# PixArt attention with a routed feed-forward: another order of TensorE's work in a half quarter, two of VectorE's groups one unit later, three small GpSimd ops left out

## The chip, the cores and the metric

The kernel runs on one core of a Trainium2 chip (trn2). The time is device microseconds of one execution. Engines are named as in the profile: PE (TensorE matmul), PEld (its weight loads), DVE (VectorE), ACT (ScalarE), POOL (GpSimd), SP (SyncE, which here issues DMAs).

## The reference, cut to what matters

There are 16 batches of 128 x 512 numbers. The first part is attention with 8 heads over the 512 positions, with keys and values both from `ctx`; the second is a feed-forward with 8 experts of which each token takes two.

```python
s = SCALE * jnp.log(k_length)[:, None, None, None]
attn = jnp.einsum('bhdq,bhdk->bhqk', qh, kh)
attn = jax.nn.softmax(s * attn, axis=-1)
out = jnp.einsum('bhqk,bhdk->bhdq', attn, vh)
...
x = x + _L0_xcond_ref(_layernorm(x, axis=-1), ctx_2048, ctx_2048, itok_B_779_1933)
x = x + _L0_ffn_ref(_layernorm(x, axis=-1), gate_w, w1, w2, w3)
```

`_layernorm` subtracts the mean of a row and divides by its standard deviation. Here x has the shape 16 x 128 x 512, HD = 128 channels, 8 heads of 16 channels, and 512 positions for queries and keys.

## The kernel before, in words

The program has two parts in time: attention for all 16 batches up to about 530 us, then the experts, tile by tile of 128 tokens. The change lies in the first.

Attention runs as a pipeline of **slots**, one per batch b (b = -3 to 17; 4 to 11 are in a hardware loop with two slots to a pass). In slot b PE computes the scores of batch b, and around it each engine prepares or finishes others: POOL splits queries of b+2 and keys of b+3 into bfloat16 parts, which go to DRAM and come back stacked; it finishes x1 (x plus attention) of b-1; it sends the tokens of b-2 to the experts' slots; and it splits one chunk of the first expert's weights.

A slot has four **quarters** (w = 0 to 3) of eight scores (u = 0 to 7), so a **half quarter** has four scores. What PE issues in a slot, all in the loop at L1096 to L1158:
- 16 **units of rows** (`rows_unit`, L1050 to L1063): two matmuls of 96 rows by 512 into `rows` (two buffers of two banks). A unit i belongs to k = (i + 4) % 16 of the next batch, from i = 12 on of the one after it. DVE takes the maximum over the keys of each row (`maxima`, L773), and unit i may start only when the maxima of unit i-2 are done. Unit 4 and unit 12 first wait for a reload (L243) of the stacked parts.
- 32 **scores** (L1076), each 128 x 512 into one of two banks; ACT takes their exponent (L655), and a score waits for the exp of the score two before it.
- 8 groups of **values** (L1089): four float32 matmuls on 32 columns each, of the quarter before.
- small products in `misc`: the transposes of z (L1109), the gate's scores (L1116), the transposes for V (L1131), u (L1139), the ranks (L1146 to L1148), and the transpose of the maxima (L1155), which waits for the maxima of unit 11.

Every engine has its own instruction queue in program order, written out by hand; semaphores alone tie them. What stands around the change:
- DVE's queue in a slot: maxima of the 16 units, and between them the routing of b-2, the reciprocal of the softmax sums (`rden`, L808, behind unit 5), the statistics of x of b+3 (L816), the copies of the maxima (`mrow`, L873, L875, behind unit 11), and `bn_stats` and `bn_aggr` of `us` (L883, L889, behind unit 13), which wait for x1 from POOL.
- POOL's queue in a slot: `psc` (L459 to L462: the scale and the negated mean of batch b+2), `norm` (L468, L470) and its split (L436, L437), a weight chunk (L434, L437, and L483, the load of another), the keys' split, the tokens of b-2 (L503 to L512), then `us` times the reciprocals (L525), x1 (L528), the wait for DVE's statistics, `zsc` (L537 to L539) and z (L540). z of one slot is followed by `psc` of the next.
- SP's queue in a slot: the reload of half 1 (for unit 4), x and ctx loads, the keys' stores, the sums' round trip through DRAM (`sums`, `den`), the queries' stores, the store of the reciprocals, the reload of half 0 (for unit 12; it waits for the 16th score), `rb` (the reciprocals spread over the heads), the maxima's round trip, and `cv`.

ACT's queue has the exps and at the end of a slot the copy of x1 (L702), which waits for POOL's L528.

`ENGINE_STEPS` (L19) tells how many steps of POOL a semaphore counts in a slot.

Of the kernel before, what the change touches and what calls it, by code (L numbers as in the profile page):

```python
# [7 lines left out]
ALU = mybir.AluOpType  # L8
# [7 lines left out]
P = 128  # L16
LOOP_FIRST, LOOP_LAST = 2, 6
LEAD = 4
ENGINE_STEPS = {"prep": 10, "keys": 4, "z": 4, "route_a": 3, "route_b": 3}  # L19
# [39 lines left out]
def build(nc, x, ctx_kv, lengths, wpack, gate_t, out):  # L59
    B, HD, L = x.shape  # L60
# [4 lines left out]
    D = L  # L65
# [25 lines left out]
    with ExitStack() as cx:  # L91
# [10 lines left out]
        xres = sb("xres", [P, B, L], F32)  # L102
# [21 lines left out]
        us = sb("us", [P, L], F32)  # L124
        rb = sb("rb", [P, L], F32)
        z = sb("z", [P, 2, ROW], F32)
        zt = sb("zt", [P, KD, P], F32)
        selu = sb("selu", [P, 2, P], F32)
        den = sb("den", [P, 32], F32)
# [267 lines left out]
        def _(pool):  # L397
# [49 lines left out]
            def slot(b):  # L447
                pbt = b.plus(2)
                if pbt.within(0, B - 1):
# [12 lines left out]
                    st.step(g.tensor_scalar(psc[:, 3:4], mean, -1.0, 0.0, ALU.mult, ALU.add))  # L462
# [4 lines left out]
                if pbt.within(1, B - 1):  # L467
                    st.step(g.tensor_tensor(norm[:, :], xres[:, bass.ds(pbt.n, 1), :].rearrange("p o q -> p (o q)"),  # L468
                                            psc[:, 3:4].to_broadcast([P, L]), ALU.add))
# [52 lines left out]
                if pv.within(0, B - 1):  # L522
# [16 lines left out]
                    st.step(g.tensor_scalar(zsc[:, 2:3], mv2[:, 0:1], -1.0, 0.0, ALU.mult, ALU.add))  # L539
                    st.step(g.tensor_scalar(z[:, pv.parity, 0:D], us[:, :], zsc[:, 2:3], zsc[:, 1:2], ALU.add, ALU.mult))  # L540
# [199 lines left out]
        def _(dve):  # L740
# [20 lines left out]
            def slot(b):  # L761
# [42 lines left out]
                if pv.within(0, B - 1):  # L804
                    dve.wait_ge(S["den_in"], b.n * 16)
                    if pv.within(1, B - 1):
                        dve.wait_ge(S["rec_out"], b.n * 16 - 16)
                    v.reciprocal(rden[:, :], den[:, :]).then_inc(S["rec_ready"], 1)  # L808
# [12 lines left out]
                maxima(range(6, 8))  # L821
# [31 lines left out]
                if b.within(-3, -3):  # L853
# [3 lines left out]
                    q_steps.step(v.tensor_scalar(us[:, :], xres[:, 0, :], psc[:, 3:4], psc[:, 2:3], ALU.add, ALU.mult))  # L857
# [5 lines left out]
                    v.nop().then_inc(S["prep_steps"], ENGINE_STEPS["prep"] - 4)  # L863
# [13 lines left out]
                maxima(range(12, 13))  # L877
                maxima(range(13, 14))
# [11 lines left out]
                maxima(range(14, 15))  # L890
# [149 lines left out]
        def _(pe):  # L1040
# [4 lines left out]
            def slot(b):  # L1045
# [53 lines left out]
                for w in range(4):  # L1099
                    for u in range(8):  # L1100
                        if u % 4 == 0:
                            rows_unit(4 * w + u // 2)
# [17 lines left out]
                        if u in (1, 5):  # L1120
                            kk = u // 4
                            if w == 0 and behind:
                                values(pv, 3, kk)
                            if w > 0 and full:
                                values(b, w - 1, kk)
# [31 lines left out]
                        if u % 4 == 3:  # L1157
                            rows_unit(4 * w + u // 2)  # L1158
# [122 lines left out]
```

## Time and profile before

| what | value |
|---|---|
| median of 3 runs (lowest, highest) | 1180.6 us (1180.52, 1184.16) |
| the profiled execution: its own time | 1181.91 us |
| the profiled execution: span | 1180.4 us, granted TensorE clock 0.957 |
| busy over the span: PE, PEld, DVE | 1039.7, 415.4, 685.0 us |
| busy over the span: ACT, POOL | 426.6, 653.9 us |
| maxima (DVE L773), 256 | 304.9 us, 1219 ns each |
| exps (ACT L655), 512 | 283.5 us, 596 ns each |

A page of the profile tells busy time of each engine, the chain of work that ended last, and groups of instructions by line. Busy time of PE is modelled: consecutive matmuls overlap, so the time from one start to the next tells more than the duration. A bracket such as [0.70 <-DVE nm L773] behind a row of the timeline is idle time of that engine just before the instruction, and what ended it.

### The profile page before, as it was taken

To read this page: it belongs to the slowest core of one execution; us is meant where nothing else is said; L and a number is where in the kernel's file an instruction comes from. 1 tells how busy PE (TensorE), PEld (TensorE's weight loads), DVE (VectorE), ACT (ScalarE), POOL (GpSimd) and SP (SyncE) were. 2 spreads that over 40 slices of the span, in tenths; PEclk is the share of its full clock that TensorE was granted. 3 is DMA by queue.
4 is the path that set the end of the run, shared out by engine and by line. 5 is a ranking of instruction groups with operands and counts; after the bars stand their busy time and mean duration, and the time that the engine had idled before them with its cause. 6 is when DMAs were issued, how large, how long until landed. Compare 5 with 4: busy or idle time off the path is not lost.

```text
span 1180.4 us, 20555 instructions
## 1 busy us (share of the span) xinstructions
PE 1039.7 (88%) x5098; PEld 415.4 (35%) x5099; DVE 685.0 (58%) x1029; ACT 426.6 (36%) x751; POOL 653.9 (55%) x618
## 2 busy tenths in 40 slices
PE   1899998989898999871799999999999999999980
PEld 0223333323232333220344444444444444444430
DVE  5867777767776777414354546535464455543356
ACT  8267776767676777751111111111101111111110
POOL 5454777676767675223287806618384383810475
PEclk9799999999999999995899999999999999999995
DMA  6575656666656554002797755737676475843778
GB/s 192 166 217 151 189 177 175 180 180 181 180 167 185 151 169 135 30 31 68 201 229 183 208 161 146 222 89 216 175 189 193 98 206 152 227 89 81 167 191 283
DMA packets 212715, 195.70 MB, mean 166 GB/s; under 512 B 137376, under 2 KB 176288, under 8 KB 207264
## 3 DMA queue, kind: packets, MB, share of 16 engines
q1 hardware_dynamic: 197760, 122.26, 40.4%
q0 software_dynamic: 14336, 71.87, 18.7%
q10 hardware_dynamic: 576, 1.05, 0.3%
q8 instruction: 19, 0.31, 0.1%
q14 instruction: 24, 0.20, 0.0%
HBM read 111.48 MB, written 53.00 MB: 139 GB/s over the span
## 4 chain that ended last, share of the span: by engine, by line
PE 66%; DMA 11%; issue 7%; POOL 6%; DVE 6%; ACT 2%; POOLq 1%; SPq 1%; DVEq 0%
PE rows L1175 30%; PE heads_out L1175 14%; PE heads_out L1089 6%; PE scores L1076 6%; PE rows L1062 5%; DMA rb<-recips_dram 4%; DMA W<-parts_dram 4%; DVE nm L773 3%; PE misc L1139 2%; ACT W L655 1%; POOL us L525 1%; POOL us L528 1%; POOLq L595 1%; PE misc L1131 1%; POOL W L598 1%
## 5 line engine op out<-in xcount | busy, mean ns | idle before, releaser
L1175 PE MATMUL rows<-W,U 128*128 (+1 forms) x1776 | 391.5, 381 | 17.3 <-DMA U<-stage 17.0
L773 DVE TENSOR_REDUCE nm<-rows 128x2 f32<-128x1024 f32 x256 | 304.9, 1219 | 98.8 <-PE rows L1062 91.6
L655 ACT ACTIVATE W<-scores 128x512 f32<-128x512 f32 x512 | 283.5, 596 | 148.0 <-PE scores L1076 146.7
L1175 PEld LDWEIGHTS rows<-W,U 128*128 128x128 bf16 x1776 | 174.2, 98 | 228.6 <-issue 21.4
L720 ACT ACTIVATE U<-rows 128x512 f32<-128x512 f32 x78 | 46.3, 597 | 509.8 <-PE rows L1175 497.9
L1175 PE MATMUL heads_out<-W,U 128*128 x888 | 199.4, 381 | 2.3 <-DMA U<-U 2.1
L1062 PE MATMUL rows<-W,U 96*128 96x512 bf16 x512 | 148.1, 399 | 56.1 <-DMA W<-parts_dram 28.2
L980 DVE TENSOR_TENSOR U<-rows,U 128x512 bf16<-128x512 f32 x78 | 53.9, 691 | 229.2 <-ACT U L720 229.0
L1076 PE MATMUL scores<-U,W 128*128 128x512 bf16 x512 | 170.7, 390 | 5.8 <-ACT W L655 5.1
L437 POOL TENSOR_TENSOR W<-U,W 128x2048 bf16<-128x2048 f32 x42 | 171.6, 4085 | 7.7 <-POOL W L436 7.7
L436 POOL TENSOR_SCALAR W<-U 128x2048 bf16<-128x2048 f32 x42 | 80.8, 1923 | 147.6 <-PE rows L1175 139.3
L1089 PE MATMUL heads_out<-W,U 128*32 128x512 f32 x1024 | 139.4, 617 | 0.5 <-ACT W L655 0.5
L1175 PEld LDWEIGHTS heads_out<-W,U 128*128 128x128 bf16 x888 | 87.3, 98 | 108.7 <-issue 5.5
L1076 PEld LDWEIGHTS scores<-U,W 128*128 128x128 bf16 x512 | 45.6, 101 | 162.6 <-ACT W L655 131.9
L1062 PEld LDWEIGHTS rows<-W,U 96*128 96x128 bf16 x512 | 46.2, 99 | 131.6 <-DVE nm L773 57.9
L906 DVE TENSOR_TENSOR stage<-stage 128x512 bf16<-128x512 f32 x39 | 83.8, 2148 | 12.4 <-ACT stage L713 12.4
L598 POOL DMA_INDIRECT W<-expert_out_dram,fidx x24 | 24.1, 1003 | 79.3 <-issue 74.5
L984 DVE TENSOR_TENSOR rows<-rows,U 128x512 f32<-128x512 f32 x78 | 54.6, 700 | 11.6 <-DVE U L980 8.9
L988 DVE TENSOR_TENSOR U<-rows,U 128x512 bf16<-128x512 f32 x78 | 54.0, 692 | 11.7 <-DVE rows L984 8.9
L548 POOL DMA_DIRECT2D U<-wpack_dram x42 | 24.0, 572 | 41.7 <-POOL W L437 23.4
L512 POOL DMA_INDIRECT slots_dram<-z,routed x32 | 33.3, 1040 | 20.0 <-POOL chosen L506 14.1
L902 DVE TENSOR_SCALAR U<-heads_out,gates 128x512 f32<-128x512 f32 x39 | 29.3, 751 | 24.2 <-PE heads_out L1175 14.7
(170 smaller groups left out, 718.9 us busy)
## 6 DMA issues: line engine op xcount, KB each, us to landing
U<-wpack_dram POOLq DMA_DIRECT2D x42, 1024.0 KB, 5.9
parts_dram<-U SPq DMA_DIRECT2D x32, 384.0 KB, 4.1
U<-parts_dram SPq DMA_DIRECT2D x32, 384.0 KB, 4.0
W<-parts_dram SPq DMA_DIRECT2D x32, 384.0 KB, 5.1
stage<-slots_dram SPq DMA_DIRECT2D x39, 257.0 KB, 3.0
expert_out_dram<-U SPq DMA_DIRECT2D x39, 256.0 KB, 3.1
parts_dram<-U SPq DMA_DIRECT2D x32, 256.0 KB, 4.0
stage<-wpack_dram POOLq DMA_DIRECT2D x12, 512.0 KB, 6.3
```

The costliest lines, as they stand in the source:

```text
L436: steps.step(g.tensor_scalar(dst_hi, src, 1.0, 0.0, ALU.mult, ALU.add))
L437: steps.step(g.tensor_tensor(tmp if tmp is not None else dst_lo, src, dst_hi, ALU.subtract))
L655: s.activation(probs[:, w % 2, j, kk, :], sc[u % 2][:, :], ACT.Exp) \
L773: v.tensor_reduce(nm[:, bb.parity, 2 * k:2 * k + 2], p1[k % 2][:, :].rearrange("p (c k) -> p c k", c=2), AX_X, ALU.max, negate=True).then_ ...
L906: v.tensor_tensor(xb[:, 1, :], xrow[:, par, 0:D], xb[:, 0, :], ALU.subtract).then_inc(S["x_lo"], 1)
L980: v.tensor_tensor(hb[:, n, 0, :], gated, silu, ALU.mult).then_inc(S["h_hi"], 1)
L984: v.tensor_tensor(gated, gated, silu, ALU.mult).then_inc(S["h_ready"], 1)
L988: v.tensor_tensor(hb[:, n, 1, :], gated, hb[:, n, 0, :], ALU.subtract).then_inc(S["h_lo"], 1)
L1062: ins = m.matmul(p1[k % 2][:, c * 512:(c + 1) * 512], qs[0:KROWS, bb.parity, hh, q0:q0 + P], ks[0:KROWS, bb.parity, hh, :], start=True, st ...
L1076: m.matmul(sc[u % 2][:, :], ks[:, b.parity, h, kc * P:(kc + 1) * P], qs[:, b.parity, h, :], start=True, stop=True).then_inc(S["scores_read ...
L1089: ins = m.matmul(ob[32 * j:32 * j + 32, :], vt[:, bb.parity, kc, 4 * (w // 2) + j, :], probs[:, w % 2, j, kk, :], start=(kc == 0), stop=(k ...
L1175: ins = m.matmul(bank, part_of(s_part, k), W[:, bass.ds(at_w, 512)], start=(k == 0 and n == 0), stop=(k == n_chunks - 1 and n == 2))
```

## The change

It does four things.

1. PE's half quarter: before, it was unit, score, score, values, score, score, unit, and so two units stood side by side. Now it is unit, score, values, score, unit, score, score. The small products keep their places behind their scores (a product at u = 4 now comes ahead of the values).
2. DVE's reciprocal moves from behind unit 5 to behind unit 6.
3. DVE's statistics of `us` (L883, L889) move from behind unit 13 to behind unit 14.
4. POOL no longer writes the negated mean: L462 and L539 are left out, in each batch's preparation and each z, and L468, L540 and DVE's L857 subtract the mean itself. Counting the first batch's own preparation apart from the others, these are three uses.

```diff
-ENGINE_STEPS = {"prep": 10, "keys": 4, "z": 4, "route_a": 3, "route_b": 3}
+ENGINE_STEPS = {"prep": 9, "keys": 4, "z": 3, "route_a": 3, "route_b": 3}
...
-                    st.step(g.tensor_scalar(psc[:, 3:4], mean, -1.0, 0.0, ALU.mult, ALU.add))
...
                     st.step(g.tensor_tensor(norm[:, :], xres[:, bass.ds(pbt.n, 1), :].rearrange("p o q -> p (o q)"),
-                                            psc[:, 3:4].to_broadcast([P, L]), ALU.add))
+                                            mean.to_broadcast([P, L]), ALU.subtract))
...
-                    st.step(g.tensor_scalar(zsc[:, 2:3], mv2[:, 0:1], -1.0, 0.0, ALU.mult, ALU.add))
-                    st.step(g.tensor_scalar(z[:, pv.parity, 0:D], us[:, :], zsc[:, 2:3], zsc[:, 1:2], ALU.add, ALU.mult))
+                    st.step(g.tensor_scalar(z[:, pv.parity, 0:D], us[:, :], mv2[:, 0:1], zsc[:, 1:2], ALU.subtract, ALU.mult))
...
                 maxima(range(4, 6))
-                if pv.within(0, B - 1):
-                    dve.wait_ge(S["den_in"], b.n * 16)
...
-                    v.reciprocal(rden[:, :], den[:, :]).then_inc(S["rec_ready"], 1)
...
-                maxima(range(6, 8))
+                maxima(range(6, 7))
+                if pv.within(0, B - 1):
+                    dve.wait_ge(S["den_in"], b.n * 16)
...
+                    v.reciprocal(rden[:, :], den[:, :]).then_inc(S["rec_ready"], 1)
+                maxima(range(7, 8))
...
-                    q_steps.step(v.tensor_scalar(us[:, :], xres[:, 0, :], psc[:, 3:4], psc[:, 2:3], ALU.add, ALU.mult))
+                    q_steps.step(v.tensor_scalar(us[:, :], xres[:, 0, :], mv1[:, 0, 0:1], psc[:, 2:3], ALU.subtract, ALU.mult))
...
-                maxima(range(12, 13))
-                maxima(range(13, 14))
+                maxima(range(12, 15))
                 if pv.within(0, B - 1):
                     dve.wait_ge(S["x1_ready"], b.n)
...
-                maxima(range(14, 15))
                 maxima(range(15, 16))
...
                         if u % 4 == 0:
-                            rows_unit(4 * w + u // 2)
+                            rows_unit(4 * w + 2 * (u // 4))
                         if full:
                             score(w, u)
...
-                        if u in (1, 5):
-                            kk = u // 4
-                            if w == 0 and behind:
-                                values(pv, 3, kk)
-                            if w > 0 and full:
-                                values(b, w - 1, kk)
...
-                        if u % 4 == 3:
-                            rows_unit(4 * w + u // 2)
+                        if u in (0, 4):
+                            kk = u // 4
+                            if w == 0 and behind:
+                                values(pv, 3, kk)
+                            if w > 0 and full:
+                                values(b, w - 1, kk)
+                        if u % 4 == 1:
+                            rows_unit(4 * w + 2 * (u // 4) + 1)
```

PE before, around the transpose of the maxima of one slot (L1155, `nm`): units 11 and 12 side by side (the `rows` row x4), and later units 13 and 14. `scores` is L1076, `heads_out` the values.

```order
-L1076 MATMUL scores<-U,W 128x512 x2
-L1062 MATMUL rows<-W,U 128x512 x4
-L1076 MATMUL scores<-U,W 128x512
-L1155 MATMUL misc<-ident,nm 128x128
-L1076 MATMUL scores<-U,W 128x512
-L1089 MATMUL heads_out<-W,U 32x512 x4
-L1076 MATMUL scores<-U,W 128x512 x2
-L1062 MATMUL rows<-W,U 128x512 x4
-L1076 MATMUL scores<-U,W 128x512 x2
```

PE now, at the same place (the lines are those of the changed file: L1073 scores, L1059 rows, L1086 values, L1146 the transpose):

```order
+L1059 MATMUL rows<-W,U 128x512 x2
+L1073 MATMUL scores<-U,W 128x512 x2
+L1059 MATMUL rows<-W,U 128x512 x2
+L1073 MATMUL scores<-U,W 128x512
+L1146 MATMUL misc<-ident,nm 128x128
+L1086 MATMUL heads_out<-W,U 32x512 x4
+L1073 MATMUL scores<-U,W 128x512
+L1059 MATMUL rows<-W,U 128x512 x2
+L1073 MATMUL scores<-U,W 128x512 x2
+L1059 MATMUL rows<-W,U 128x512 x2
```

No two units stand side by side any more: two scores are between unit 11 and unit 12, and values between the first score of a half and its second.

DVE before, from the copies of the maxima (`mrow`) on; the two reductions ahead of BN_STATS are units 12 and 13, those behind it unit 14 and on:

```order
-L875 TENSOR_TENSOR mrow<-misc,mrow 32x128
-L771 REGISTER_ALU
-L772 ISA
-L773 TENSOR_REDUCE nm<-rows 128x2
-L772 REGISTER_ALU
-L773 TENSOR_REDUCE nm<-rows 128x2
-L883 BN_STATS st<-us 128x6
-L889 BN_AGGR mv<-st 128x2
-L772 REGISTER_ALU
-L773 TENSOR_REDUCE nm<-rows 128x2
```

DVE now:

```order
+L874 TENSOR_TENSOR mrow<-misc,mrow 32x128
+L769 REGISTER_ALU
+L770 ISA
+L771 TENSOR_REDUCE nm<-rows 128x2
+L770 REGISTER_ALU
+L771 TENSOR_REDUCE nm<-rows 128x2
+L770 REGISTER_ALU
+L771 TENSOR_REDUCE nm<-rows 128x2
+L881 BN_STATS st<-us 128x6
+L887 BN_AGGR mv<-st 128x2
```

One more reduction stands ahead of the statistics.

## Rows read from the trace of the kernel before

**Rows 1.** Windows: us, busy us (instructions) of each engine, granted clock, DMA share, GB/s.

```profile
core 0: us, PE busy (x) PEld busy (x) DVE busy (x) ACT busy (x) POOL busy (x), PEclk, DMA share, GB/s
180.00:405.00 225.00, 203.16 (x1111) 68.62 (x1112) 163.43 (x222) 151.94 (x286) 157.00 (x201) 0.98 0.60 175
```

**Rows 2.** Waits in 101 to 405: who <- for whom: us, times, longest.

```profile
PE rows L1062 <- DVE nm L773: 17.8, 19, 1.8
POOL zsc L537 <- DVE mv L889: 17.7, 10, 3.6
```

**Rows 3.** Timeline, PE: start, us, instruction, [idle before <- releaser]. Slots 7 to 9.

```profile
286.38 0.61 PE L1062 MATMUL rows<-W,U 96*128 96x512 bf16 x2 [0.54 <-DVE nm L773]
...
302.40 0.60 PE L1062 MATMUL rows<-W,U 96*128 96x512 bf16 x2 [0.70 <-DVE nm L773]
...
309.60 0.33 PE L1155 MATMUL misc<-ident,nm 128*128 128x128 f32 x1 [0.65 <-DVE nm L773]
...
316.78 0.64 PE L1062 MATMUL rows<-W,U 96*128 96x512 bf16 x2 [1.79 <-DVE nm L773]
...
334.39 0.61 PE L1062 MATMUL rows<-W,U 96*128 96x512 bf16 x2 [0.70 <-DVE nm L773]
```

**Rows 4.** Timeline, POOL, slot 8 into slot 9.

```profile
313.22 1.27 POOL L528 TENSOR_TENSOR us<-xres,us 128x512 f32<-128x512 f32 x1 [0.28 <-POOL us L525]
316.04 0.19 POOL L537 TENSOR_SCALAR zsc<-mv 128x1 f32<-128x1 f32 x1 [1.54 <-DVE mv L889]
...
317.18 0.19 POOL L539 TENSOR_SCALAR zsc<-mv 128x1 f32<-128x1 f32 x1 [0.20 <-POOL zsc L538]
...
320.51 0.19 POOL L462 TENSOR_SCALAR psc<-mv 128x1 f32<-128x1 f32 x1 [0.20 <-POOL psc L461]
```

**Rows 5.** Timeline, POOL's x1 in slots 1, 11, 12, 14; last row by lines, 101 to 405.

```profile
100.87 1.28 POOL L528 TENSOR_TENSOR us<-xres,us 128x512 f32<-128x512 f32 x1 [0.18 <-POOL us L525]
...
404.93 1.27 POOL L528 TENSOR_TENSOR us<-xres,us 128x512 f32<-128x512 f32 x1 [0.27 <-POOL us L525]
...
433.75 1.27 POOL L528 TENSOR_TENSOR us<-xres,us 128x512 f32<-128x512 f32 x1 [0.18 <-POOL us L525]
...
490.02 1.26 POOL L528 TENSOR_TENSOR us<-xres,us 128x512 f32<-128x512 f32 x1 [0.18 <-POOL us L525]
...
L525 POOL TENSOR_TENSOR us<-us,rb 128x512 f32<-128x512 f32 x10 | 12.8, 1279 | 2.5 <-DMA rb<-recips_dram 2.4
```

**Rows 6.** Chain that ended last, slot 9: start, us, what.

```profile
321.16 0.22 PE scores L1076
321.38 0.45 PE rows L1062 x2
```

**Rows 7.** Chain that ended last, a half quarter of slot 15.

```profile
509.05 1.00 PE heads_out L1089 x8
510.04 0.34 PE scores L1076
510.40 1.09 ACT W L655 x2
511.54 0.39 PE scores L1076
```

**Rows 8.** Timeline, DVE, slot 11 at the statistics of `us`.

```profile
405.67 1.23 DVE L773 TENSOR_REDUCE nm<-rows 128x2 f32<-128x1024 f32 x1 [0.46 <-PE rows L1062]
406.81 0.69 DVE L883 BATCH_NORM_STATS2 st<-us 128x6 f32<-128x512 f32 x1
```

**Rows 9.** Windows, one microsecond behind the stall of slot 9.

```profile
318.00:319.00 1.00, 1.00 (x5) 0.20 (x8) 0.99 (x1) 0.97 (x2) 0.40 (x2) 0.50 1.10 236
```

**Rows 10.** The page's DMA issues (median us to landing), then chain pieces.

```profile
W<-parts_dram SPq DMA_DIRECT2D x32, 384.0 KB, 5.1
...
301.76 0.41 SPq L243
302.55 7.68 DMA rb<-recips_dram
...
333.75 7.49 DMA W<-parts_dram
```

More of the change, by code:

```diff
@@ L803, in slot @@
                 maxima(range(4, 6))
-                if pv.within(0, B - 1):
-                    dve.wait_ge(S["den_in"], b.n * 16)
-                    if pv.within(1, B - 1):
-                        dve.wait_ge(S["rec_out"], b.n * 16 - 16)
-                    v.reciprocal(rden[:, :], den[:, :]).then_inc(S["rec_ready"], 1)
                 lb = b.plus(3)
@@ L820, in slot @@
                     v.bn_aggr(mv1[:, lb.parity, :], st1[:, :]).then_inc(S["st1_ready"], 1)
-                maxima(range(6, 8))
+                maxima(range(6, 7))
+                if pv.within(0, B - 1):
+                    dve.wait_ge(S["den_in"], b.n * 16)
+                    if pv.within(1, B - 1):
+                        dve.wait_ge(S["rec_out"], b.n * 16 - 16)
+                    v.reciprocal(rden[:, :], den[:, :]).then_inc(S["rec_ready"], 1)
+                maxima(range(7, 8))
                 if routes:
@@ L862, in slot @@
                     q_steps.end()
-                    v.nop().then_inc(S["prep_steps"], ENGINE_STEPS["prep"] - 4)
+                    v.nop().then_inc(S["prep_steps"], ENGINE_STEPS["prep"] - 3)
                     v.nop().then_inc(S["prep_done"], 1)
```

## The prediction, made before the changed kernel ran

> **What bounds the kernel now.** First the windows view: in the steady stretch from 180 to 405 us PE is busy 203.2 of 225 us and POOL 157.0 [rows 1]. PE looks like the bound, yet it stands still about 20 us there, so next comes the view of waits: PE's units of rows wait 17.8 us for DVE's maxima in 19 places, and POOL waits 17.7 us in 10 places for the statistics `mv` [rows 2]. The timeline of one slot, number 8, shows where PE stands: before unit 8 (0.70), before the transpose of the maxima (0.65), and before unit 0 of the next slot (1.79) [rows 3]. The last is the large one and has a long cause. DVE's queue has `bn_stats` of `us` ahead of the maxima of unit 14; that waits for POOL's x1 (L528), whose end is 313.22 + 1.27 = 314.49 [rows 4]. Unit 0 starts at 316.78, 2.3 us after it. So I follow POOL: L528 starts at 100.87 in slot 1 and at 404.93 in slot 11, ten links of 30.4 us, while the next link takes 28.8 and the two after it 28.1 each [rows 5].
>
> Is POOL's pass closed in itself? In the ten links POOL waits for nothing from PE except `rb` (2.4 us in all [rows 5]). Its other gaps are 0.2 to 1 us between its own instructions, and its wait for `mv` is 1.54 us of unavoidable DVE work where DVE stands ready [rows 4]. Some 30 us of POOL instructions and hand-overs follow one another, z to the next z. **POOL's chain is the bound from slot 1 to slot 11; PE is pulled along by it** through the `bn_stats` in DVE's queue. After slot 11 POOL no longer splits weights and the slots near PE's own pace.
>
> **The change, part by part** (sum against the profiled execution, 1181.9 us; the median of the runs shown is 1180.6).
>
> *Three small POOL ops.* L539 takes 0.19 us with 0.20 idle ahead of it, L462 the same [rows 4]. One of each lies in every link, so a link loses 2 x 0.39 = 0.78 us; ten links: 7.8 us. The subtraction that replaces them is done in instructions that were there with the same shape, whose cost I leave as it is. The third removal is the copy of the same negation that feeds DVE's first group; it has no row of its own, and lies in the start. The Trainium skill (Perfetto Trace Analysis, Identifying the Most-Contended Engine) says to take the engine with the highest occupancy first; by it these ops, on an engine busy 157 of 225 us, would be worth nothing and PE's idle time everything. I go by the chain instead, and keep that reading as a rival.
>
> *PE's order.* Before, units are issued in pairs and the second of a pair comes right behind the first; now a unit is followed by score, values, score (0.22 + 0.99 + 0.32 us), then the second unit, then two scores. The work of a half quarter stays: two units of 0.45, four scores of 0.22 (0.34 right behind values), one group of values of 1.00 [rows 6, 7]. What moves: (1) unit 8 needs the maxima of unit 6, which get 1.5 us more, so the 0.70 goes. (2) the transpose needs unit 11's maxima; unit 11 now ends 1.1 us before it instead of 0.65, so 0.65 becomes about 0.2. (3) the 1.79: see below. What it adds: score 3 needs the exp of score 1, which now comes only 0.65 us ahead, against an exp of 0.60; I charge 0.05 us per half quarter, 0.4 a slot (bounds 0 and 0.8, as the exps of a pair take 1.09 [rows 7]).
>
> *Statistics one unit later.* Now unit 14's maxima come first, and the unit held up by x1 is unit 1 of the next slot, not unit 0. Call the end of x1 T. Unit 1 starts at T + 2.3. Slot 8 goes from unit 0 (286.38) to unit 8 (302.40) in 16.0 us [rows 3]; without the 0.70, and starting 2.0 us further on, unit 8 is reached at T + 15.6, the transpose at T + 22.2, and unit 14's maxima end 4.7 us later (three maxima of 1.23 each [rows 8], two short copies and the hand-overs) at T + 26.9. The next x1 ends at T + 29.5. So DVE still stands ready when x1 comes, POOL is not held up, and PE has some 2 us of slack in each pass. Where PE still has a stall of 1.8 its clock may fall again: in 318 to 319 it was granted at 0.50, that is 1.2 GHz, after the 1.79 us stall [rows 9]; the slot with this fall takes 32.0 us from unit 8 to unit 8 (302.40 to 334.39 [rows 3]), the mean link 30.4. Another 1.6 us puts unit 14's maxima at T + 28.5, still in time.
>
> *Reciprocal one unit later.* It used to follow unit 5's maxima and now unit 6's; but unit 6 now stands where unit 5 stood behind PE's u product. Its time in PE's order does not move. Behind it wait SP's store of the reciprocals and the `rb` load. `rb` took 7.68 us to land [rows 10] and in some slots POOL waits for it. With PE a unit further on against x1 and no fall of the clock it comes earlier, so the 2.4 us go.
>
> *DMAs.* The reload for unit 12 is issued at 301.76 in slot 8 [rows 10], 17.7 us after T (286.38 less 2.3). It waits for the 16th score on PE and for the landing of the stored queries; with PE earlier and POOL 0.8 earlier I put it at T + 16.7. It took 5.1 us in the median and 7.5 at its longest here [rows 10], and PE would be there at T + 21.4. So a stall of 0.4 us, at worst 2.8, appears before unit 12. It takes from PE's slack only; at worst unit 14's maxima end at T + 29.8, 0.3 late.
>
> *Sum.* Slots 1 to 11: 7.8 (ops) + 2.4 (`rb`) + 0.5 (two links in which DVE came late to x1, as at 406.81 against the end of x1 at 406.20 [rows 5, 8]) = 10.7. Slots 11 to 14: the first link 28.8 - 0.78 - 0.61 = 27.4; in the next two POOL has less to do and PE sets the pace: 28.1 less 0.70, less 0.45, less 0.25 of what remains of PE's stalls, plus 0.4 = 27.1. Together 85.1 becomes 81.6: 3.5. Slot 15 has no units; its half quarters run values 1.00, score 0.34, exps 1.09, score 0.39, in 2.9 us [rows 7]. With values between the scores I count about 0.1 less each; I take 0.5 of 1.0 for eight, and 0.4 for the op before the last z: 0.9. Start: in slots 0 and 1 PE waits for reloads, and unit 15 now comes ahead of the score that starts one: plus 0.4 to 0.9, half covered, so -0.5. The experts' part begins when attention ends and has the same instructions: nothing. 10.7 + 3.5 + 0.9 - 0.5 = **14.6 us**. 1181.9 - 14.6 = 1167.3; on the median 1180.6 - 14.6 = **1166.0**.
>
> **The rivals.**
> - *DVE comes late to x1, and it gets slower.* Place: `bn_stats` behind unit 14. Price: POOL waits up to one maximum, 1.23 us, per link, against 0.78 saved: +0.45 for 13 links, +6, and `rb` keeps its waits: 1187. It decides where unit 14's maxima end over 0.8 us after x1, that is, where PE's transpose comes later than T + 25.5. For: in slot 1 POOL's wait for `mv` was 3.6 us [rows 2], as DVE was late. Against: 3 us of margin in the steady slots. 4%.
> - *It cancels.* The same in half the links and the reload late in all: gain 0 to 3.5, 1179. 5%.
> - *Part of it.* The ops count, but new stalls for reloads or ACT keep slots 11 to 15 as they are and `rb` late: 7.8 + 1 = 9, 1172. 16%.
> - *PE is the bound after all.* Then its stalls of 17.8 us in ten slots go [rows 2], three falls of the clock with 1.6 us each too, and 3.5 + 0.9 - 0.5 behind: 26.6 us, 1154. This is the time by the page's reading of occupancy. The trace speaks against it, since PE's largest stall ends 2.3 us behind an instruction of POOL in slot after slot. 7%.
> - *The forecast*, 1162 to 1170: 68%.
>
> **How the numbers follow.** The likeliest case gives 1166.0. The range reaches down to 1160 (PE's slots after 11 faster, the start free) and up to 1175 (the third rival and a few late statistics). A measurement of this kernel can tell about 0.3%, 3.5 us, from no change. Faster by more: 68 + 16 + 7 = 91%; within: 5%; slower: 4%.
>
> **What would show it.** The two small ops gone and the starts of x1 29.5 us apart from slot 1 to 11 (about 295 us for ten links against 304); POOL's wait for `mv` still 1.5 us; no wait of POOL for `rb`; the stall before unit 8 gone, that before the transpose about 0.2; PE's large stall now before unit 1, or before unit 12 for the reload; links of 27 us after slot 11; the part from 560 us on as long as before. It is wrong if POOL's wait for `mv` grows above 2.3, if x1 comes every 30 us or more, or every 28.

## The result, and the profile after

| | before | after |
|---|---|---|
| median (lowest, highest) | 1181.91 us of 4 runs (1180.52, 1184.16) | 1197.14 us of 4 runs (1195.09, 1202.57) |
| the profiled execution: its own time | 1181.91 us | 1195.09 us |
| the profiled execution: span, granted clock | 1180.4 us, 0.957 | 1193.2 us, 0.954 |

The ratio is 1.0134, with a 95% interval of [1.0093, 1.0176]: **the change makes the kernel slower by 1.3%**, where 1.2% faster was forecast. The sign is wrong, by more than the 0.3% that the prediction takes for telling a change from none, and the time lies outside its range of 1160 to 1175 us.

The first view is the one of a single line, that of GpSimd's z, in the kernel after and in the kernel before. The first row has the shortest, median and longest duration in ns:

```profile
L538 POOL TENSOR_SCALAR z<-us,mv,zsc x16: 2071/2072/2085, 105.1 to 552.0; 128x512 f32<-128x512 f32 x16
```

```profile
L540 POOL TENSOR_SCALAR z<-us,zsc x16: 761/762/767, 107.3 to 540.2; 128x512 f32<-128x512 f32 x16
```

The shape, the types and the second operation are the same. Only `add` became `subtract`, and the instruction takes 2.07 us instead of 0.76: 1.31 us more, against 0.39 us saved by the op left out ahead of it. The timeline of POOL from slot 8 into slot 9 shows where that lies; it answers to [rows 4]:

```profile
319.39 1.26 POOL L527 TENSOR_TENSOR us<-xres,us 128x512 f32<-128x512 f32 x1 [0.28 <-POOL us L524]
322.19 0.18 POOL L536 TENSOR_SCALAR zsc<-mv 128x1 f32<-128x1 f32 x1 [1.54 <-DVE mv L887]
322.57 0.57 POOL L537 TENSOR_TENSOR zsc<-zsc,mhalf 128x1 f32<-128x1 f32 x1 [0.19 <-POOL zsc L536]
323.36 2.07 POOL L538 TENSOR_SCALAR z<-us,mv,zsc 128x512 f32<-128x512 f32 x1 [0.22 <-POOL zsc L537]
...
327.69 1.04 POOL L467 TENSOR_TENSOR norm<-xres,mv 128x512 f32<-128x512 f32 x1 [0.27 <-POOL psc L461]
```

The other subtraction that the change brought, in `norm` (L467), takes 1.04 us, and so it is not at fault. A link of POOL's chain gets 2 x 0.39 us shorter and 1.31 longer: +0.53 us, in ten links 5.3. The starts of x1, answering to [rows 5], show more than that (slots 1, 11 and 14):

```profile
99.55 1.26 POOL L527 TENSOR_TENSOR us<-xres,us 128x512 f32<-128x512 f32 x1 [0.18 <-POOL us L524]
...
415.15 1.26 POOL L527 TENSOR_TENSOR us<-xres,us 128x512 f32<-128x512 f32 x1 [0.26 <-POOL us L524]
...
501.33 1.26 POOL L527 TENSOR_TENSOR us<-xres,us 128x512 f32<-128x512 f32 x1 [0.18 <-POOL us L524]
```

Ten links take 315.6 us instead of 304.1, that is 31.6 each and 11.5 in all. The other 6.2 us are waits of POOL. The view of waits from 101 to 405 us, which answers to [rows 2], has most of them, and what PE waits for:

```profile
PE misc L1106 <- POOLq L540: 12.1, 10, 1.9
PE rows L1059 <- DVE nm L771: 2.9, 4, 0.8
...
POOL zsc L536 <- DVE mv L887: 20.3, 10, 3.3
...
POOL z L502 <- DVEq L840: 3.3, 3, 1.7
...
POOL us L524 <- DMA rb<-recips_dram: 2.5, 1, 2.5
```

From the x1 of slot 1 to that of slot 11, POOL waits 2.53 us longer than before for the statistics `mv`, 1.14 longer for `rb` (2.5 us in this view and 1.0 right behind it), and 2.54 longer ahead of L502, where it takes over VectorE's routing of a batch: before, it never waited for VectorE there, now it does in three slots. These are the 6.2 us. VectorE's queue, with the reciprocal that `rb` needs in it, goes by the maxima of PE's units, so the next question is what PE does.

PE's wait for the maxima fell from 17.8 to 2.9 us, as wanted. A new wait of 12.1 us stands in its place: line 1106, the transposes of z. Before, unit 0 stood behind x1, and when PE came to the transposes, z was there. Now PE comes early and z comes late. The timeline of PE shows what follows:

```profile
322.95 0.60 PE L1059 MATMUL rows<-W,U 96*128 96x512 bf16 x2 [0.73 <-DVE nm L771]
323.39 0.38 PE L1073 MATMUL scores<-U,W 128*128 128x512 bf16 x1
325.62 1.12 PE L1106 MATMUL misc<-ident,z 128*128 128x128 f32 x4 [1.84 <-POOLq L540]
326.95 1.06 PE L1059 MATMUL rows<-W,U 96*128 96x512 bf16 x2 [0.22 <-issue]
```

z ends at 323.36 + 2.07 = 325.43, and the transposes start at 325.62. Four transposes take 1.12 us there. The windows view (columns as in [rows 1]) has the clock behind this stall, and the whole stretch:

```profile
326.00:328.00 2.00, 1.78 (x7) 1.11 (x7) 0.00 (x0) 1.08 (x2) 1.25 (x4) 0.50 1.07 381
...
332.00:334.00 2.00, 2.00 (x6) 0.79 (x5) 0.76 (x1) 1.41 (x3) 1.74 (x2) 0.50 0.00 0
334.00:336.00 2.00, 2.00 (x12) 1.00 (x14) 2.00 (x2) 1.35 (x3) 1.64 (x1) 0.57 0.03 8
```

```profile
180.00:405.00 225.00, 206.06 (x1037) 73.73 (x1058) 161.51 (x210) 145.98 (x272) 156.78 (x178) 0.92 0.55 166
```

PE was granted half speed, 1.2 GHz, from 326 to 334 us and for most of the two microseconds behind. The transposes of z stall 1.84 or 1.85 us in slots 5, 7, 9 and 11 (at 197.5, 261.6, 325.6 and 390.1) and 0.6 in those between. Added up over windows of one microsecond, the clock is at half for 6.8, 10.2, 10.2 and 6.8 us in these four slots, from 199.2, 260.6, 325.5 and 390.3 on, and PE is late for all that follows. (In the kernel before, three falls of 3.4 us each lie in the same stretch.) That shows where x1 next needs VectorE, in slot 7:

```profile
286.27 3.59 DVE L771 TENSOR_REDUCE nm<-rows 128x2 f32<-128x1024 f32 x3
289.78 0.68 DVE L881 BATCH_NORM_STATS2 st<-us 128x6 f32<-128x512 f32 x1
```

x1 ended at 288.01 there, so that its statistics began 1.77 us late; in slots 9 and 11 it was 1.77 and 1.11. Over the stretch from 180 to 405 the clock is 0.92 instead of 0.98 [rows 1], and PE is busy longer (206.1 us) with fewer instructions (1037).

The ledger of the two profiled executions: start -1.3 (100.87 to 99.55); ten links +11.5; slots 11 to 14 +1.1 (85.1 to 86.2); slot 14's x1 to the end of the span +1.5 (690.4 to 691.9). That is +12.8, which is the difference of the spans. The matmuls of the experts take 584.9 us from first to last instead of 583.4.

### The profile page after: what moved, and what is told of

Its sections match the earlier page's. It is cut to its first block, busy times and chain, and to the rows that moved or that the text cites. A ratio compares the mean times of both kernels' runs of the same rounds, so it can differ in the third digit from the quotient of the medians.

```text
span 1193.2 us, 20372 instructions
## 1 busy us (share of the span) xinstructions
PE 1052.2 (88%) x4995; PEld 422.8 (35%) x5099; DVE 698.1 (59%) x1029; ACT 428.9 (36%) x751; POOL 668.6 (56%) x586
## 4 chain that ended last, share of the span: by engine, by line
PE 66%; POOL 10%; DMA 7%; issue 7%; DVE 5%; ACT 2%; POOLq 2%; SPq 1%; DVEq 0%; ACTq 0%
PE rows L1172 30%; PE heads_out L1172 14%; PE heads_out L1086 6%; PE scores L1073 6%; PE rows L1059 5%; DVE nm L771 3%; POOL z L538 2%; DMA rb<-recips_dram 2%; PE misc L1130 2%; DMA W<-parts_dram 2%; PE misc L1113 1%; ACT W L653 1%; PE misc L1106 1%; POOL W L596 1%; DVE st L881 1%
## 5 line engine op out<-in xcount | busy, mean ns | idle before, releaser
L653 ACT ACTIVATE W<-scores 128x512 f32<-128x512 f32 x512 | 293.5, 599 | 149.4 <-PE scores L1073 140.1
L1172 PE MATMUL heads_out<-W,U 128*128 x868 | 196.7, 379 | 3.4 <-DVE U L899 2.3
L1059 PE MATMUL rows<-W,U 96*128 96x512 bf16 x512 | 166.7, 410 | 36.5 <-DMA W<-parts_dram 27.2
L1073 PE MATMUL scores<-U,W 128*128 128x512 bf16 x466 | 181.3, 394 | 10.8 <-ACT W L653 6.3
L1086 PE MATMUL heads_out<-W,U 128*32 128x512 f32 x1024 | 140.7, 622 | 2.0
L1073 PEld LDWEIGHTS scores<-U,W 128*128 128x128 bf16 x512 | 49.3, 98 | 216.8 <-ACT W L653 151.7
L1059 PEld LDWEIGHTS rows<-W,U 96*128 96x128 bf16 x512 | 49.3, 102 | 84.1 <-issue 33.1
```

The costliest lines, as they stand in the source:

```text
L653: s.activation(probs[:, w % 2, j, kk, :], sc[u % 2][:, :], ACT.Exp) \
L1059: ins = m.matmul(p1[k % 2][:, c * 512:(c + 1) * 512], qs[0:KROWS, bb.parity, hh, q0:q0 + P], ks[0:KROWS, bb.parity, hh, :], start=True, st ...
L1073: m.matmul(sc[u % 2][:, :], ks[:, b.parity, h, kc * P:(kc + 1) * P], qs[:, b.parity, h, :], start=True, stop=True).then_inc(S["scores_read ...
L1086: ins = m.matmul(ob[32 * j:32 * j + 32, :], vt[:, bb.parity, kc, 4 * (w // 2) + j, :], probs[:, w % 2, j, kk, :], start=(kc == 0), stop=(k ...
L1172: ins = m.matmul(bank, part_of(s_part, k), W[:, bass.ds(at_w, 512)], start=(k == 0 and n == 0), stop=(k == n_chunks - 1 and n == 2))
```

## The experiments

Each ratio is against the kernel before, measured beside it. The first theory was that the slow form of z explains the loss alone. Its rival was that the new order, with the wait it brings, costs time by itself.

**Only z back as it was.** The change, but with L539 there and z adding:

```diff
-st.step(g.tensor_scalar(z..., us, mv2[:, 0:1], zsc[:, 1:2], ALU.subtract, ALU.mult))
+st.step(g.tensor_scalar(zsc[:, 2:3], mv2[:, 0:1], -1.0, 0.0, ALU.mult, ALU.add))
+st.step(g.tensor_scalar(z..., us, zsc[:, 2:3], zsc[:, 1:2], ALU.add, ALU.mult))
```

> The changed kernel with z computed as before: the small op zsc<-mv is back, and z adds the negated mean. Everything else of the change stays (PE's order, both VectorE groups, the small psc op left out). Theory A (the z instruction with subtract as its first operation takes 2.07 us against 0.76, and nothing else costs): z is back at 0.76, a link of POOL falls by 2.07 - 0.76 - 0.39 = 0.92 us against the changed kernel, in 16 links 15 us, and where PE waited for z (14.8 us in 13 places) that goes too with the falls of the clock behind it: 1168 to 1174 us. Theory B (PE's new order is the cause, since its half quarter now takes 3.05 us where 2.83 was counted): z at 0.76 but slots 12 to 14 stay at 29 us each and the total stays above 1185.

Measured: 1174.13 us, ratio 0.9930 [0.9905, 0.9954]. The ends of x1 go from 99.70 in slot 1 to 395.50 in slot 11, 29.6 us a link. Without the two edits in z the change gains 8.8 us.

**z alone.** The kernel before with the opposite edit, L539 out and z subtracting (`"z": 3`).

> The kernel before with one edit: z subtracts the mean itself and the small op zsc<-mv is left out. PE's and VectorE's orders are those of before. Theory A: z takes 2.07 us, a link 0.92 us more in 16 links, 10 to 15 us in all, so 1191 to 1197. Theory B: the long z is hidden and the time stays within 4 us of before.

Measured: 1191.43 us, ratio 1.0083 [1.0061, 1.0106]; links of 30.95 us. The form of z costs 8.5 us in the old order. The two parts do not add: -8.8 and +8.5 make -0.3, and the whole change was measured at +15.2. **About 15 us come only of the two together.** With the slow z in the old order PE's stalls for z are at most 0.32 us from slot 1 to 14, with z back in the new order at most 0.92, and with both up to 1.85, three of the four largest with half speed right behind and one with half speed 1.7 us later.

**Order and groups alone.** The kernel before with the change's hunks in TensorE's order and VectorE's two groups, and GpSimd's ops as they were.

> The kernel before with PE's new order and both VectorE groups one unit later; every GpSimd instruction as before. Theory A: POOL's links stay near 30.1 us without waits for rb, so slots 1 to 11 gain 0 to 3 us; slots 12 to 14 take 29.0 instead of 28.2, a loss of 2; in all 1178 to 1183. Theory B: most of the loss is here, above 1190.

Measured: 1181.0 us, ratio 0.9988 [0.9974, 1.0003], no difference. Links of 30.4 us as before; POOL's chain sets them. The loss of 2 us behind slot 11 that was expected isn't there: the three links from slot 11 to 14 take 82.2 us against 85.1.

**The op in the preparation alone.** The kernel before without L462 and with `norm` subtracting (`"prep": 9`).

> The kernel before with one edit: the small psc op is left out and norm subtracts the mean itself (tensor_tensor with a broadcast mean, 1.04 us in both kernels). By both theories 0.38 us for each of 11 or 12 links on POOL's chain: 4 to 5 us faster, 1176 to 1177.

Measured: 1174.48 us, ratio 0.9939 [0.9918, 0.9959], links of 29.66. That is twice the gain expected, 0.74 us off a link for an op of 0.39. In the ten links POOL's timeline has 7.4 us less: 4.4 for the op and its hand-over, 2.4 for the wait for `rb`, which is gone, and 0.4 for the statistics. The clock from 180 to 405 us is 1.00 instead of 0.98.

**Is it the operation or the operand?** Two kernels, run once each: the change, with one word of z altered, so that it adds the mean where it should subtract it; and the kernel before, with a copy of the mean where the negation was, so that z subtracts from the same column that it added before.

```diff
-st.step(g.tensor_scalar(z..., us, mv2[:, 0:1], zsc[:, 1:2], ALU.subtract, ALU.mult))
+st.step(g.tensor_scalar(z..., us, mv2[:, 0:1], zsc[:, 1:2], ALU.add, ALU.mult))
```

> The changed kernel with one word of z changed: the first operation adds the mean from mv2 instead of subtracting it (so x1 is normalised with the wrong sign of the mean, and the routing sees that). If subtract as the operation makes z slow, z takes 0.76 us here; if it is that its two column operands come from two tiles (mv2 and zsc), z stays at 2.07 us.

```diff
-st.step(g.tensor_scalar(zsc[:, 2:3], mv2[:, 0:1], -1.0, 0.0, ALU.mult, ALU.add))
-st.step(g.tensor_scalar(z..., us, zsc[:, 2:3], zsc[:, 1:2], ALU.add, ALU.mult))
+st.step(g.tensor_scalar(zsc[:, 2:3], mv2[:, 0:1], 1.0, 0.0, ALU.mult, ALU.add))
+st.step(g.tensor_scalar(z..., us, zsc[:, 2:3], zsc[:, 1:2], ALU.subtract, ALU.mult))
```

> The kernel before, where the small op copies the mean instead of negating it, and z subtracts that copy from the tile zsc. Both column operands of z come from one tile, as before. If subtract is what costs, z takes 2.07 us and the time is that of z alone changed plus 16 small ops, 1193 to 1199; if the operands' place is, z stays at 0.76 and the time near before.

Measured: 1167.79 us, with z at 762 ns, for the first; 1199.82 us, with z at 2076 ns, for the second, 0.8 above its range. The word `subtract` is the cause of the slow z. The tile that it reads is not.

**The forms by themselves.** 16 instructions at the end of GpSimd's program:

```diff
+pr.step(g.tensor_scalar(rest, norm, c0, c1, ALU.add, ALU.mult))        # L629
+pr.step(g.tensor_scalar(rest, norm, c0, c1, ALU.subtract, ALU.mult))   # L630
+pr.step(g.tensor_scalar(rest, norm, c1, c0, ALU.mult, ALU.subtract))   # L631
+pr.step(g.tensor_scalar(rest, norm, c1, c0, ALU.mult, ALU.add))        # L632
+pr.step(g.tensor_scalar(rest, norm, 0.5, 2.0, ALU.subtract, ALU.mult)) # L633
+pr.step(g.tensor_scalar(rest, norm, 0.5, 2.0, ALU.add, ALU.mult))      # L634
+pr.step(g.tensor_tensor(rest, norm, c0.to_broadcast, ALU.subtract))    # L635
+pr.step(g.tensor_tensor(rest, norm, c0.to_broadcast, ALU.add))         # L636
```

> The kernel before, with 16 instructions of GpSimd on tiles of 128x512 float32 added at the end of its program, twice each: tensor_scalar with two columns as add and mult, subtract and mult, mult and subtract, mult and add; with two constants as subtract and mult, add and mult; and tensor_tensor with a column broadcast, as subtract and as add. If the subtraction of tensor_scalar is what is dear on GpSimd: 2.07 us for the forms with subtract and 0.76 us for those without, tensor_tensor 1.04 us in both. If only a subtraction that comes first is: mult and subtract 0.76 us as well. If only one by a column is: the form with constants 0.76 us or less. The total is about 20 us above the kernel before or, where these instructions lie beside other work, less.

The timeline of POOL in the second round, in which each instruction follows the one before it:

```profile
1184.02 0.77 POOL L629 TENSOR_SCALAR rest<-norm,zsc 128x512 f32<-128x512 f32 x1 [0.22 <-POOL rest L636]
1185.00 2.07 POOL L630 TENSOR_SCALAR rest<-norm,zsc 128x512 f32<-128x512 f32 x1 [0.21 <-POOL rest L629]
1187.28 2.08 POOL L631 TENSOR_SCALAR rest<-norm,zsc 128x512 f32<-128x512 f32 x1 [0.21 <-POOL rest L630]
1189.57 0.77 POOL L632 TENSOR_SCALAR rest<-norm,zsc 128x512 f32<-128x512 f32 x1 [0.21 <-POOL rest L631]
1190.53 1.93 POOL L633 TENSOR_SCALAR rest<-norm 128x512 f32<-128x512 f32 x1 [0.20 <-POOL rest L632]
1192.66 0.62 POOL L634 TENSOR_SCALAR rest<-norm 128x512 f32<-128x512 f32 x1 [0.20 <-POOL rest L633]
1193.46 1.04 POOL L635 TENSOR_TENSOR rest<-norm,zsc 128x512 f32<-128x512 f32 x1 [0.18 <-POOL rest L634]
1194.67 1.04 POOL L636 TENSOR_TENSOR rest<-norm,zsc 128x512 f32<-128x512 f32 x1 [0.18 <-POOL rest L635]
```

Every `tensor_scalar` with a subtraction in it, first or second, by a column or by a constant, takes 1.30 or 1.31 us more than its twin with an addition. `tensor_tensor` takes the same for both. The kernel's time in its one execution was 1205.93 us, 24 above before.

**A version that keeps the gain.** VectorE negates the mean behind its `bn_aggr`, and GpSimd's z adds it. First in the old order:

```diff
 v.bn_aggr(mv2[:, :], st2[:, :]).then_inc(S["st2_ready"], 1)
+dve.wait_ge(S["st2_ready"], b.n)
+v.tensor_scalar(nmean[:, :], mv2[:, 0:1], -1.0, None, ALU.mult).then_inc(S["nmean_ready"], 1)
...
+hold(S["nmean_ready"], pv.n + 1)
+st.step(g.tensor_scalar(z..., us, nmean[:, 0:1], zsc[:, 1:2], ALU.add, ALU.mult))
```

> The kernel before with the small psc op left out (as in the run of that alone, 1174.5 us) and the small zsc op moved to VectorE: behind bn_aggr VectorE writes the negated mean of 128x1, and GpSimd's z adds it with its old operation. If GpSimd's chain is the bound, 0.39 us per link go again, 10 links and part of the later ones: 4 to 6 us, 1169 to 1171. If TensorE sets the pace by now, VectorE's longer queue costs and nothing is gained: 1174 to 1176.

Measured: 1173.43 us, ratio 0.9923 [0.9904, 0.9942], between the two cases of the expectation; links of 29.6, hardly shorter than with L462 alone out. In the old order PE still waits 16.3 us for the maxima from 101 to 405 us, and the second op bought next to nothing. POOL's timeline shows where its 3.9 us in ten links went: z starts 0.34 us behind the op ahead of it instead of 0.22 (1.3 us in ten), the waits for `rb` and for the statistics are 1.2 us longer, the rest is in small gaps. Then with the whole change:

> The whole change, with the subtraction in z written as an addition: VectorE multiplies the mean by -1 into a column of its own behind its bn_aggr (one more instruction of 128x1 there), and z adds that column. Theory (the time was lost by the form of GpSimd's z alone, and the rest of the change does what was forecast): z takes 0.76 us, x1 comes every 29.2 us, and the time is 1167 to 1170. Rival (the new order costs PE about 3 us in the half quarters, so that the order is worth nothing over the old one with the same links of GpSimd): 1173 to 1175, as in the run with the old order and VectorE's negation.

Measured: **1171.28 us, ratio 0.9915 [0.99, 0.993]**. z takes 762 ns, and the links are 29.46, not 29.2. The time lies between the theory's 1167 to 1170 and the rival's 1173 to 1175. This is the version of this study that beats both kernels and computes the same. The windows view of 180 to 405 us:

```profile
180.00:405.00 225.00, 214.52 (x1170) 73.44 (x1173) 177.80 (x238) 160.06 (x301) 159.45 (x194) 1.00 0.62 184
```

The granted clock is 1.00, and PE is busy 214.5 us. Its waits for z in 101 to 405 are 3.2 us in 7 places, none over 0.5. Its parts follow.

**Groups moved, old order** (the version with VectorE's negation, TensorE's hunks undone):

> The old order of TensorE, z adding the mean that VectorE negated, L462 and L539 left out, and VectorE's two groups (reciprocal, bn_stats) one unit later as in the change. If the moved bn_stats is what frees TensorE (unit 0 no longer behind x1), the large stall goes from unit 0 to unit 1 and the time is 1168 to 1171. If it is TensorE's order that gains, it stays at 1173 to 1174; if the pair of units then stands behind x1 with bn_stats between unit 15's maxima, nothing moves: 1173 to 1175.

Measured: 1206.18 us, ratio 1.0203 [1.0157, 1.025], over 30 us above every case of the expectation. The queue of SP, slot 7:

```profile
287.64 0.33 SPq L293 DMA_DIRECT2D recips_dram<-rden  x1
288.40 0.35 SPq L244 DMA_DIRECT2D U<-parts_dram  x1
```

The 16th score was at 286.11, and the reload (L244) should follow it. In the full version it does, 0.42 us behind (slot 8: 293.80 and 294.22); here it goes 2.29 us behind, as SP's store of the reciprocals stands ahead of it in the queue and waits for a reciprocal that comes one unit later. The view of waits on PE from 101 to 405 us:

```profile
PE rows L1063 <- DMA W<-parts_dram: 23.9, 10, 3.4
```

The statistics of x1 start 1.3 to 4.8 us late in every slot from 1 to 13. The two groups were not moved one by one, so that the late store accounts for the loss is read from the rows, not shown by a run.

**Order without the moved groups:**

> The new order of TensorE, z adding the mean that VectorE negated, L462 and L539 left out, and VectorE's two groups where they were before. If the order gains by itself: 1168 to 1170. If the order needs the moved groups: 1173 to 1176, with the large stall before unit 0 at some 2 us still there; if the new order costs more than it gives without them, above 1176.

Measured: 1177.54 us, ratio 0.9954 [0.9935, 0.9972], slower than with them by 6 us, and over 1176, the expectation's worst case: the order needs the groups. Its links are 30.2 in the mean, but four of them (from slot 4 to slot 8) take 31.5, 30.9, 31.7 and 31.2, and those behind 29.5 to 29.8. PE waits for the maxima 4.2 us only, but for the reload 12.0:

```profile
PE rows L1062 <- DMA W<-parts_dram: 12.0, 8, 2.4
```

In slot 7 GpSimd issues the fetch of an expert's weights at 270.40 and SP the reload of `W` at 271.22. It lands 7.88 us later, PE has waited 2.41 us for it, and 3.4 us at half speed follow. The other large stalls for the reload in this run (1.74, 1.86, 1.54, 1.35 and 1.65 us) also have the fetch ahead of the reload, by 0.7 to 1.2 us. In the full version's slot 7 the reload goes at 265.49, the fetch behind it at 265.95, and PE does not wait. In two slots the fetch was ahead by 0.6 and 0.4 us without a stall of that size. That the two transfers hinder each other fits the rows better than any other reading that I have. No run took the fetch away, so it isn't shown.

**Another spread: rows, score, score, values, rows, score, score.** With L462 out and VectorE's groups unmoved:

```diff
-    rows_unit(4 * w + u // 2)
+    rows_unit(4 * w + 2 * (u // 4))
...
-if u % 4 == 3:
-    rows_unit(4 * w + u // 2)
+if u % 4 == 1:
+    rows_unit(4 * w + 2 * (u // 4) + 1)
```

> The kernel before with the small psc op left out (alone 1174.5 us) and TensorE's half quarter in another order: rows, score, score, values, rows, score, score. Units are spread as in the change, but both scores of a pair stay side by side ahead of values. Theory: the change's order cost TensorE 0.2 us per half quarter because score 4 waits for the exp of score 2, which stands behind values; here that chain is gone, a half quarter of slots 12 to 14 takes 2.85 us instead of 3.05, and slots 12 to 14 take 27.3 to 27.8 us instead of 28.2. Total 1172 to 1174. If the spread of units itself costs, they take 28.5 or more and the total is over 1175.

Measured: 1178.73 us, ratio 0.9962 [0.9942, 0.9983]: a miss, 4 us slower than the old order without L462, with intervals that just overlap. Two things stand in its trace. PE waits for the reload (5.4 us in 6 places from 101 to 540 us, at most 2.0), as in the run before, with VectorE's groups unmoved here too. And the premise of the expectation is false: a half quarter without a stall takes neither 2.85 nor 3.05 us but 3.32 (values at 278.83 to values at 282.15). Slots 12 to 14 take 28.3 us each in the mean. How much each of the two costs wasn't tried by itself.

**Is the rest of the forecast there?** Three kernels measured side by side: the mean added (in more executions than above), the old order with VectorE's negation again, and the best version in this other spread.

> The change with z adding the mean where it should subtract it (this part of the computation is changed: z has the wrong sign of the mean), in five rounds. One look at this kernel gave 1167.8. If all terms of the forecast hold but for the form of z: 1166 to 1169. If the look was a lucky one and the order is worth nothing: 1171 to 1173.

Measured: 1168.72 us, ratio 0.9878 [0.986, 0.9895]. The forecast was 0.9876 (1166.0 over 1180.6).

> TensorE's old order and VectorE's groups where they were, L462 and L539 left out, VectorE negating the mean and z adding it: a repeat in five rounds beside the others. If TensorE's order is worth something with GpSimd's pass shortened, this stays at 1173 to 1175, at least 2 us above the run with the new order; if it is worth nothing, 1171 to 1172.

Measured: 1173.7 us, ratio 0.9926 [0.9905, 0.9947], 5 us above the mean added: the case in which the order is worth something, though these two also differ by VectorE's negation.

> The version that was to beat both (new order, VectorE negates the mean, both of its groups one unit later), with the half quarter as rows, score, score, values, rows, score, score: the exp that the third score waits for then lies behind a score that is already done, so the wait of the scores for ACT (6.7 us in 20 places) should go. If that mis-sized term is what is missing: 1167 to 1169. If the second unit behind values comes too late for VectorE, or GpSimd's pass sets the time anyway: 1171 to 1173.

Measured: 1173.9 us, ratio 0.9918 [0.9899, 0.9937]: no gain over the best version, and just above the lower of the two cases, 1171 to 1173. From 40 to 540 us the scores' wait for ACT fell only from 6.7 to 5.2 us, and PE's waits for `W` and for the maxima from 9.0 to 4.5. But this order makes PE's own work longer: a half quarter without a stall takes 3.32 us (values at 277.71 to values at 281.03), against 3.05 in the best version (272.11 to 275.16) and 2.89 in the kernel before (280.91 to 283.80). In slots 4 to 11, where POOL's chain sets the pace, the links are those of the best version (29.2 and 29.7 in turn). Behind slot 11, where PE sets it, the three links take 83.9 us against 81.7.

The starts of x1 in the run with the mean added (slots 1, 11, 14):

```profile
100.46 1.26 POOL L527 TENSOR_TENSOR us<-xres,us 128x512 f32<-128x512 f32 x1 [0.18 <-POOL us L524]
...
393.58 1.26 POOL L527 TENSOR_TENSOR us<-xres,us 128x512 f32<-128x512 f32 x1 [0.26 <-POOL us L524]
...
475.16 1.26 POOL L527 TENSOR_TENSOR us<-xres,us 128x512 f32<-128x512 f32 x1 [0.18 <-POOL us L524]
```

Ten links take 293.1 us where the forecast had 304.1 - 10.7 = 293.4, and slots 11 to 14 take 81.6 where it had 81.6.

## Why the prediction was wrong, point by point

- **The step that failed**: "The subtraction that replaces them is done in instructions that were there with the same shape, whose cost I leave as it is." For `norm` it holds (1.04 us). For z it is false: 0.76 became 2.07 us. The trace of before had no `tensor_scalar` with a subtraction on GpSimd, and so no row for its price. It was an operation that the trace did not show, and it got a price of nothing instead of two bounds. A term of 7.8 us saved in ten links was in truth 5.3 us lost: 0.78 saved and 1.31 added in each.
- **POOL's chain as the bound**: right. With z's form mended (the mean added), the sum for slots 1 to 11 came out to 0.3 us, and its terms did too: in POOL's timeline about 8.2 us for the two ops, 2.4 for `rb` and 0.4 for late statistics, against 7.8, 2.4 and 0.5. That the whole, 0.9878, meets the forecast's 0.9876 as closely as it does is luck in part. In the profiled executions, the mean-added kernel is 14.9 us ahead at slot 14's x1, where the forecast had 13.7, and loses 3.9 behind it, where the forecast had 0.9 to gain; only the median of five executions brings the gain back to 14.0.
- **PE's largest stall, "now before unit 1, or before unit 12 for the reload"**: wrong in the place, and by the traces this is what doubled the damage (11.5 us in ten links for the 5.3 of z's form). The forecast asked when unit 14's maxima would be done against x1. It did not ask when PE comes to the next thing that POOL makes, the transposes of z. In the timelines above, with T the end of x1 (320.65), unit 1 starts at T + 2.3, just as forecast, and PE is done with the score behind it at T + 3.1; z starts at T + 2.7 and would end at T + 3.5 with 0.76 us, and ends at T + 4.8 with 2.07. PE waits there even with z at 0.76 us (0.54 a slot with the mean added). At 2.07 us it is 1.84 in every second slot from 5 on, with half speed behind it.
- **The first rival** (DVE comes late to x1) happened in slots 7, 9 and 11, at 1.1 to 1.8 us each; its price had been up to 1.23 us a link, so it was worked out too small: it did not have PE at half speed. It got 4% because PE was to have "some 2 us of slack in each pass"; the stall for z and the microseconds at half speed used that up.
- **`rb`**: its waits should go, and grew (3.5 us in the ten links, in two places). With z mended and the groups moved along with the order they went down to between nothing and 1.1, nearly as forecast; in the order without the moved groups they were 4.5, and with the groups moved alone 5.9.
- **0.05 us per half quarter** for the score that waits for ACT: mis-sized. In the timeline of after, a half quarter without a stall (values at 279.11 to values at 282.16) takes 3.05 us, against 2.89 before; that is 0.16 and not 0.05, some 1.3 us a slot instead of 0.4. Where POOL sets the pace it is hidden. Slots 11 to 14 still came out at 81.6 with z mended, so the stalls that went there must have been worth about 0.9 us a slot more than the 1.4 counted: two sizes that were off and cancel.
- **Slot 15, 0.9 us to gain**: not there. From the end of slot 14's x1 to the start of the last z it takes 49.9 us with the mean added and 49.9 in the best version, against 48.9 before: 1.0 us longer instead of 0.9 shorter.
- **The start, -0.5**: x1 of slot 1 started 0.4 us earlier than before with the mean added, 1.5 in the best version and 2.4 with z back. But the kernels with PE's old order and VectorE's groups unmoved lie between 1.8 us earlier and 0.7 later themselves, so this gain can't be put down to the change.
- **The experts' part**, "nothing": in the profiled executions its matmuls took 582.3 to 589.5 us from first to last. The longest is that of the best version, against 583.4 before. From slot 14's x1 to the end of the span it takes 690.4 us before, 694.2 with the mean added and 696.3 in the best version; 1 us of this lies in slots 15 and 16, and no run shows what the rest is.
- **Rival "PE is the bound"**: no. The Trainium skill (Perfetto Trace Analysis, Identifying the Most-Contended Engine) has one optimize first the engine with the highest occupancy. The prediction took PE's 203 of 225 us for that. The same section, though, does not judge TensorE by its matmul busy time but by its share of peak rate and by its weight loads, here 68.6 of 225 us [rows 1]; the first of these the profile doesn't give. Of the others VectorE, busy 163.4, stands just ahead of GpSimd's 157.0, so that rule does not name GpSimd either. The run that helped only PE and its partners gave 0.9988; the one that took a single 0.19 us op from GpSimd, busy 157, gave 0.9939. The measurement decides here: the chain that closes on itself bound the time, at an occupancy of 70%.
- **What PE's order is worth** once POOL's chain is short is small in the whole time: 1171.28 against 1173.43 and 1173.7, with intervals that overlap ([0.99, 0.993] against [0.9904, 0.9942] and [0.9905, 0.9947]). Those of the mean added and of the old order do not overlap. Up to the x1 of slot 14 it is more: it starts at 475.6 us in the profiled execution of the best version, against 481.6 and 480.2 in those of the old order, and what follows takes 696.3 us against 692.4 and 690.3. So 14.0 us were measured only with the wrong sign of the mean, 10.8 with the right one. Of the 3 us between, the ten links have 1.5, of which 1.2 stand right ahead of z (0.34 us each instead of 0.22) and 0.35 are waits for the statistics; the rest stays open.

## What to carry to other kernels

An edit that swaps one operation for another "in the same instruction" is a new instruction: if the trace has no row of that engine, operation and shape, bound its price from both sides, and where the operand can be negated elsewhere for next to nothing, add instead. When an order is changed so that an engine stands still less, follow it to the next thing that it must wait for; two edits of which one makes a consumer early and the other its producer late can cost more than their sum, here 15 us more. Parts that were moved together may only work together: take each out before calling one of them useful.

## What the runs showed of the hardware that I had not expected

- GpSimd's `tensor_scalar` on 128x512 float32 takes 0.76 us as add and mult with columns and 0.62 with constants, but 2.07 and 1.93 with a subtraction in either place. `tensor_tensor` takes 1.04 us as add and as subtract.
- In the changed kernel, stalls of PE of 1.84 or 1.85 us, three of the four with one of 0.73 to 0.81 shortly ahead, were followed by 6.8 or 10.2 us at half speed. In the kernel before, stalls of 1.82, 1.79 ([rows 3], [rows 9]) and 1.78 us were each followed by 3.4 us at half speed, and one of 1.76 (at 194.83) by none. With a stall for z of at most 0.54 us in a slot, and none over 1.0 of any kind, it was 1.00 from 180 to 405 us.
